# Moving a graph kernel's self loop from TensorE products to GpSimd edits of the resident adjacency

## What is computed

```
L0: dis*(adj @ (dis*h)) - h + sigmoid(alpha) * (softmax(beta*cosine*adj) @ h - h)
L1: (adj @ h + beta*h) / (deg + beta) @ kernel + bias
L2: relu((adj + I) normalised by its row sums @ (h @ W) + b)      <- the self loop I
L3: h_mul(concat(h, exp_map(adj @ log_map(h_mul(h, embed) + ...))), layer) + ...
```

## Time and profile before

| | |
|---|---|
| median of 3 runs | 905.12 us |
| the profiled execution | 904.95 us, of which 903.2 us is its span |
| TensorE busy | 849.7 us (94%) |
| VectorE, ScalarE, GpSimd busy | 626.5, 487.1, 289.5 us |
| mean granted TensorE clock | 0.991 of full speed |

### The profile page before, as it was taken

One profiled execution on the slowest core, in us unless ns is written; L12 is line 12 of the kernel. 1 busy time (PEld: TensorE's weight loads), 2 busy tenths in 40 slices (PEclk: granted clock), 3 DMA queues, 4 the chain that ended last, 5 costly groups with the idle time before them and its releaser, 6 DMA issues.

```text
span 903.2 us, 18349 instructions
## 1 busy us (share of the span) xinstructions
PE 849.7 (94%) x6464; PEld 510.3 (57%) x6464; DVE 626.5 (69%) x1775; ACT 487.1 (54%) x1027; POOL 289.5 (32%) x381
## 2 busy tenths in 40 slices
PE   0699999999999999999999999999999999999992
PEld 0366777777777777654444455555455555555451
DVE  6989999999999999953444313313147676637776
ACT  5878888888888886731222111111055566434543
POOL 6844444444654464531221100000022131213221
PEclk9999999999999999999999999999999999999997
DMA  8999999999999994000000000000000000000000
GB/s 262 223 224 271 234 269 232 282 232 254 258 271 249 240 249 111 2 1 1 1 1 0 1 1 1 1 1 1 1 1 1 1 1 1 1 1 25 24 24 25
DMA packets 96080, 89.79 MB, mean 99 GB/s; under 512 B 74368, under 2 KB 79616, under 8 KB 96000
## 3 DMA queue, kind: packets, MB, share of 16 engines
q1 hardware_dynamic: 92352, 88.11, 41.2%
q10 hardware_dynamic: 3648, 0.61, 0.4%
HBM read 69.81 MB, written 2.10 MB: 80 GB/s over the span
## 4 chain that ended last, share of the span: by engine, by line
PE 70%; DVE 15%; issue 6%; ACT 3%; DVEq 2%; POOL 2%; DMA 1%; ACTq 1%; SPq 0%; POOLq 0%
PE ps_acc L1353 28%; PE ps_acc L1264 16%; PE ps_s L1247 10%; PE ps_t L1353 6%; PE ps_t L1247 5%; DVE e_parts L803 2%; DVE ps_s L796 2%; POOL att_sb L385 1%; ACT e_parts L612 1%; DVE adj_t L735 1%; PE ps_s L1383 1%; PE ps_s L1415 1%; DMA x<-in_x 1%; PE ps_acc L1341 1%; ACT ez L571 1%
## 5 line engine op out<-in xcount | busy, mean ns | idle before, releaser
L334 POOL CAST e_parts<-ez 128x512 f16<-128x512 f32 x256 | 158.2, 645 | 177.5 <-ACT ez L483 116.1
L1264 PEld LDWEIGHTS ps_acc<-h_a,e_parts 128*128 128x128 f16 x3072 | 185.8, 97 | 34.4 <-DVE e_parts L803 4.2
L1264 PE MATMUL ps_acc<-h_a,e_parts 128*128 128x129 f16 x3072 | 197.4, 219 | 2.5 <-DVE e_parts L803 2.3
L1353 PE MATMUL ps_acc<-adj_t,stage 128*128 128x512 fp8e4 x896 | 198.6, 379 | 0.0
L803 DVE TENSOR_TENSOR e_parts<-ez,e_parts 128x512 f16<-128x512 f32 x256 | 180.0, 744 | 1.0 <-POOL e_parts L334 1.0
L1353 PE MATMUL ps_acc<-adj_t,h_a 128*128 128x512 fp8e4 x768 | 170.3, 379 | 0.0
L1353 PEld LDWEIGHTS ps_acc<-adj_t,stage 128*128 128x128 f16 x896 | 87.1, 98 | 99.1
L1247 PE MATMUL ps_s<-u_t 128*128 128x512 f16 x534 | 132.3, 385 | 9.0 <-ACT ez L483 7.3
L458 ACT ACTIVATE bytes<-stage 128x1024 uint8<-128x1024 f32 x128 | 133.8, 1046 | 0.9 <-DVE x L764 0.7
L483 ACT ACTIVATE ez<-ps_s,scal 128x1024 f32<-128x1024 f32 x89 | 107.1, 1203 | 44.4 <-DVE ps_s L796 43.3
L571 ACT ACTIVATE ez<-x,small 128x128 f32 (+1 forms) x96 | 39.6, 482 | 155.4 <-DVE small L980 155.4
(11 more groups left out here) (157 smaller groups left out, 814.4 us busy)
## 6 DMA issues: line engine op xcount, KB each, us to landing
stage<-in_adj SPq DMA_DIRECT2D x128, 512.0 KB, 5.0
x<-in_x SPq DMA_DIRECT2D x4, 512.0 KB, 8.5
adj_t<-bytes SPq DMA_TRANSPOSE x128, 5.1
out<-x SPq DMA_DIRECT2D x8, 256.0 KB, 2.2
kernel_sb<-in_L_gnn_kernel ACTq DMA_DIRECT2D x1, 64.0 KB, 7.1
w_sb<-in_L_gnn_W ACTq DMA_DIRECT2D x1, 64.0 KB, 8.1
embed_top<-in_L_gnn_embed ACTq DMA_DIRECT2D x1, 64.0 KB, 8.4
embed_top<-in_L_gnn_layer ACTq DMA_DIRECT2D x1, 64.0 KB, 7.3
```

The costliest lines, as they stand in the source:

```text
L334: g.tensor_copy(e_parts[:, HI, at, :], ez[:, at, :]).then_inc(ehi_done, 1)
L1264: last = t.matmul(att_acc[:, b, 0:D + 1], e_parts[:, re, g_s % RING, P * b:P * (b + 1)], h_a[:, s, rh, 0:D + 1], start=(s == 0 and n == 0 ...
L1353: last = t.matmul(acc, h[:, k, r, :], adj_f8[:, k // 2, CW * c:CW * (c + 1), k % 2], start=(k == 0 and r == LO), stop=(k == NB - 1 and r = ...
```

## The change

The products with `ident16x2` are taken out of `aggregate`. GpSimd adds the identity times 2.0 to the diagonal blocks of `adj_f8` after layer 1 has read them, so that an entry on the diagonal becomes 4.0, and subtracts it after layer 2 has read them. Each chunk is four GpSimd operations of 128 by 128 with an fp8 input and output and an fp16 identity. TensorE waits for the add at quarter (c, c) of layer 2, and for the subtraction at quarter (c, c) of layer 3. Two of GpSimd's loops on the chip become lists written out.

```diff
-            with pool.Fori(0, NCH) as m:
+            def self_loops(m, op, done):
+
+                for b in range(BC):
+                    k = BC * m + b
+                    own = adj_f8[:, k // 2, P * k:P * (k + 1), k % 2]
+                    last = g.tensor_tensor(own, own, ident16x2[:, :], op, saturate=False)
+                last.then_inc(done, 1)
+
+            for m in range(NCH):
                 rstd(NCH + m)
+                pool.wait_ge(agg_done, NCH + m + 1)
+                self_loops(m, ALU.add, loop_in)
...
-            with pool.Fori(0, NCH // 2 - 1) as i:
+            for i in range(NCH // 2 - 1):
                 roots_of_pair(i)
                 for par in (0, 1):
                     rstd(2 * NCH + 2 * i + 2 + par)
                     root_h(2 * i + 2 + par, par)
+                    pool.wait_ge(agg_done, 2 * NCH + 2 * i + par + 1)
+                    self_loops(2 * i + par, ALU.subtract, loop_out)
             roots_of_pair(NCH // 2 - 1)
+            pool.wait_ge(agg_done, 3 * NCH)
+            for m in (NCH - 2, NCH - 1):
+                self_loops(m, ALU.subtract, loop_out)
...
-                if L == 2 and q == NB // BC - 1:
-
-                    for b in range(BC):
-                        for r in (LO, HI):
-                            t.matmul(acc[:, P * b:P * (b + 1)], h[:, BC * c + b, r, :],
-                                     ident16x2[:, :], start=False, stop=False,
-                                     skip_group_check=True)
+                if L >= 2 and q == c:
+
+                    pe.wait_ge((loop_in, loop_out)[L - 2], c + 1)
```

More of the change, by code:

```diff
@@ L206, in program @@
                  "h_sq_in n_h_ok v_sq_in n_v_ok h2_sq_in n_h2_ok a_sq_in n_a_ok cat_sq_in "
-                 "n_cat_ok tanh_in tanh_out ln_in ln_out h2_ok v_ok v_out split_g diag_hi diag_ok "
+                 "n_cat_ok tanh_in tanh_out ln_in ln_out h2_ok v_ok v_out split_g loop_in loop_out diag_hi diag_ok "
                  "x_less x_att").split()
@@ L217, in program @@
          h_sq_in, n_h_ok, v_sq_in, n_v_ok, h2_sq_in, n_h2_ok, a_sq_in, n_a_ok, cat_sq_in,
-         n_cat_ok, tanh_in, tanh_out, ln_in, ln_out, h2_ok, v_ok, v_out, split_g, diag_hi,
+         n_cat_ok, tanh_in, tanh_out, ln_in, ln_out, h2_ok, v_ok, v_out, split_g, loop_in, loop_out,
+         diag_hi,
          diag_ok, x_less, x_att) = (
```

## The result

| | before | after |
|---|---|---|
| median of 9 runs each | 905.34 us | 903.24 us |
| ratio, 95% interval | | 0.9978 [0.9969, 0.9988] |
| the profiled execution / its span | 904.95 / 903.2 us | 903.19 / 901.2 us |

The change takes 0.22% off the time, with an interval of 0.12 to 0.31%. The forecast was 903.7; the median lies 0.46 under it, inside the range of 902.4 to 905.7, but outside the 903.4 to 904.4 that the prediction called the forecast itself. As a gain it is 2.0 us where 1.4 was forecast.

What follows compares the result with a forecast made beforehand. In layer 2 a circle through VectorE, ScalarE and GpSimd, with TensorE only in `prepare`, was taken to lead. The sum was 904.95 - 1.78 (removal) + 0.35 (collision) = 903.52 us, median 903.7, range 902.4 to 905.7.

Steps and rivals of the forecast that it cites:

- the forecast itself: Whole kernel: the median to expect lies between 903.4 and 904.4 us; chance 0.49.
- Only four of eight groups count: Layer 2, TensorE: removing identity products pays for chunks 0, 1, 2 and 7 only, 1.78 us; chunks 3 to 6 give nothing.
- VectorE's pass stays at 35.07: Layer 2: VectorE's pass over two chunks still takes 35.07 us after the change.
- The gap before `prepare(3)` grows to 1.2 us, and its start moves by 1.34: Layer 2, TensorE: it waits about 1.2 us there instead of 0.31, and the step at 711.34 moves by 1.34.
- The edit takes 0.35 us: GpSimd: one fp8 operation of 128 columns takes 0.35 us, between bounds of 0.28 and 0.56.
- The edits for an odd chunk cost nothing: Layer 2: VectorE's 2.37 us of idle time behind the root covers four operations of up to 0.56 us.
- The additions in layer 1 cost nothing: Layer 1: GpSimd's additions may delay VectorE, with 14 us of cover for at most 4 x 0.56 us.
- The collision at layer 3's start costs 0.35: Last eight GpSimd operations meet VectorE's small ones: VectorE loses 1.4 us, of which 1.05 is covered; loss 0.35 us.
- The room: Layer 3's start: VectorE's last split ends at 802.08, TensorE needs it at 803.13, 1.05 us later.
- no collision, or one inside the room: Rival, layer 3's start: GpSimd's last operations cost VectorE nothing that counts, so four groups pay in full: 903.3 us; chance 0.17.
- VectorE shut out until the last edit: Rival, layer 3's start: GpSimd's eight operations lock VectorE out throughout, costing 1.75 us: 905.1 us; chance 0.12.

Runs made afterwards that it cites:

- e2: Kernel before without the identity products of chunks 3, 4, 5 and 6, no edits on GpSimd; 905.69 us, ratio 1.0003 to before, distance on TensorE +0.02 us.
- e3: Kernel before without the identity products of chunks 0, 1, 2 and 7, no edits on GpSimd; 903.34 us, ratio 0.9982 to before, distance on TensorE -1.77 us.
- e10: Changed kernel with the last eight edits (chunks 6 and 7) held back until VectorE's last split of layer 2 is done; 903.6 us, ratio 0.9983 to before.
- e6: Changed kernel with two more GpSimd operations ahead of each chunk's four edits, written to a spare tile; 904.64 us, ratio 0.9997 to before.
- e11: e10 with ScalarE's loop of three passes in layer 2 written out; 900.72 us, ratio 0.9952 to before.
- e12: Kernel before with ScalarE's loop in layer 2 written out and nothing else; 903.84 us, ratio 0.9986 to before.
- e1: Kernel before without all eight groups of identity products in layer 2, no edits on GpSimd; 903.33 us, ratio 0.9983 to before.
- e4: Changed kernel with the identity products kept as well, so layer 2's self loop counts twice; 906.07 us, ratio 1.0008 to before.
- e5: The changed kernel again, nothing else altered; 903.4 us, ratio 0.9983 to before.
- e8: Changed kernel with prepare(3) and prepare(5) one quarter later in TensorE's list; 904.73 us, ratio 0.9994 to before.
- e7: Changed kernel with the last eight edits moved behind the first roots of layer 3, the roots' loop written out; 904.63 us, ratio 0.9995 to before.
- e9: Changed kernel with four more GpSimd operations ahead of each chunk's four edits, written to a spare tile; 908.97 us, ratio 1.0041 to before.

## Why the prediction was right, and where it was off

- **Only four of eight groups count.** Right, and shown by e2 and e3: +0.02 and -1.77 against 0 and -1.78.
- **VectorE's pass stays at 35.07.** It is 35.04, from these rows of VectorE after:

```profile
687.35 1.11 DVE L1119 SCALAR_TENSOR_TENSOR bytes<-ps_s,cols,bias_bc 128x128 f32<-128x128 f32 x4
...
722.39 1.12 DVE L1119 SCALAR_TENSOR_TENSOR bytes<-ps_s,cols,bias_bc 128x128 f32<-128x128 f32 x4
```

- **The gap before `prepare(3)` grows to 1.2 us, and its start moves by 1.34.** It is 1.17 late by the list (1.01 by the row's bracket) and moved by 1.51, of which 0.15 is the earlier start of the whole stretch.
- **The edit takes 0.35 us.** It takes 0.39: eight in a row last 3.12, four beside VectorE's small operations 1.58, and eight with VectorE idle 3.13 (e10). GpSimd's timeline of after:

```profile
697.74 2.07 POOL L403 TENSOR_TENSOR adj_t<-adj_t,ident16x 128x128 fp8e4<-128x128 fp8e4 x4
700.10 1.38 POOL L304 TENSOR_TENSOR small<-small,scal 128x4 f32<-128x4 f32 x1 [0.29 <-DVE small L984]
...
706.74 1.58 POOL L403 TENSOR_TENSOR adj_t<-adj_t,ident16x 128x128 fp8e4<-128x128 fp8e4 x4
...
793.85 3.12 POOL L403 TENSOR_TENSOR adj_t<-adj_t,ident16x 128x128 fp8e4<-128x128 fp8e4 x8
```

The block for an even chunk is the first row: it began beside VectorE's operation that ends at 698.37, and 1.44 us after that, at 699.81, it is through, close to the 1.40 that the prediction took. The root behind it was asked for 0.29 later and ended at 701.48, 0.53 before VectorE used it at 702.01. So the cost is nothing, with 0.29 + 0.53 = 0.82 us of cover for the root. e6 shows that this sum is not the whole margin: two more operations are 0.78 us, and its passes are 0.36 and 0.34 longer, 0.2 of it because VectorE's L994 itself stood behind an edit.

- **The edits for an odd chunk cost nothing.** Right: beside the block at 706.74 VectorE's L1039 took 0.39 and L1046 0.41 us instead of 0.17, but its idle time behind them, ended by ScalarE, shrank from the 2.37 of the earlier trace rows to 1.97 us.
- **The additions in layer 1 cost nothing.** Right. TensorE's timelines of before and of after, where layer 1 begins:

```profile
502.42 22.61 PE L1353 MATMUL ps_acc<-adj_t,h_a 128*128 128x512 fp8e4 x104
```

```profile
502.27 22.61 PE L1365 MATMUL ps_acc<-adj_t,h_a 128*128 128x512 fp8e4 x104
```

From there to 624.52 and to 624.37 it is 122.10 us in both.

- **The collision at layer 3's start costs 0.35.** This is the term that was mis-sized: VectorE's loss was put at 1.4 us and measured 1.04. The mechanism came as described, VectorE's timeline of after:

```profile
793.91 0.39 DVE L1039 TENSOR_SCALAR att_sb<-att_sb 128x8 f32<-128x8 f32 x1 [2.74 <-POOL att_sb L386]
...
794.76 0.20 DVE L1044 RECIPROCAL att_sb<-att_sb 128x8 f32<-128x8 f32 x1
795.05 0.40 DVE L1046 SCALAR_TENSOR_TENSOR att_sb<-att_sb 128x8 f32<-128x8 f32 x1
...
796.57 0.42 DVE L1056 SCALAR_TENSOR_TENSOR att_sb<-att_sb 128x8 f32<-128x8 f32 x1
...
797.31 0.69 DVE L1150 TENSOR_TENSOR ez<-ez,att_sb 128x512 f32<-128x512 f32 x1
...
800.44 0.69 DVE L1002 TENSOR_TENSOR h_a<-ez,h_a 128x512 f16<-128x512 f32 x1
```

Its stretch lasts 801.13 - 793.91 = 7.22 us, against 6.18 in e10 and before. It lost 1.04 us, not 1.4, because it was held up six times and not eight, by 0.17 on average: the reciprocals (L1044 above), for one, took 0.20 with and without the edits. The room was 1.05, so the loss just fits. TensorE's block of 24 took 5.39 instead of 5.34 (5.34 in e10, too), so 0.05 came through, not 0.35.

- **The number.** What came true at layer 3's start is the rival *no collision, or one inside the room*, put at 903.3 with a chance of 0.17; the median is 903.24. For the profiled execution the sum gave 903.52, and 903.19 was measured, 0.33 less. Of this 0.30 is the collision. Another 0.27 came off by the start of the stretch (0.15), the tail (0.07) and 0.05 in the stretch, all of the size of the scatter, and 0.24 came on outside the span, for which the prediction had no term. That these last nearly cancel is luck. The other 0.13 of the 0.46 is the distance from the profiled execution to its median: 0.17 was taken, it is 0.05 in after.

- **VectorE shut out until the last edit** (the rival with the lock in its harshest form) did not come: 3.12 us of edits back to back cost it 1.04. The Trainium skill (SBUF — State Buffer, Who interferes with whom) calls the port an exclusive lock whose loser blocks fully. The rows agree for a VectorE instruction that meets one edit (L1039, 0.39 instead of 0.17); by them VectorE gets its turn between two edits, and some of its instructions, such as L1044, are not held up at all.

## What to carry to other kernels

A busy share of 99.8% does not make an engine the bound: look for the one step at which it stands waiting, however short, because a circle through the other engines that is just as long as its list will swallow whatever you take out of the list. Sort the work that a change removes by whether it lies inside such a circle, and test it by taking out one half at a time (e2 and e3). Then look for what can leave the circle; here that was a table load, worth 0.80 us before the change and 2.6 after it.

## What the runs showed of the hardware

- The loop on the chip costs ScalarE a table load of 1.28 us ahead of its first plain copy in a pass; in the written-out passes it is absent (L594 with its load at 707.89 and without one at 777.75 above, L595 in e11). That it is the loop which makes the load necessary is shown by e11 and e12; why it stands just there was not tested.
- VectorE operations on eight columns with one tensor input are held up by a running GpSimd operation too: L1039 took 0.39 us beside the edits, and 0.17 in e10 (L1040 there), where there were none. Not all are: the reciprocal L1044 took 0.20 beside them, as in e10.
- GpSimd is held up as well: the block of four at 697.74 took 2.07 us. VectorE had begun an operation of 512 columns at 697.68 that lasts 0.69, to 698.37. The block at 706.74 met only operations on eight columns and took 1.58.
- The time outside the span is 0.2 us longer in after: 1.98 us as the mean of its nine executions, against 1.79 in before (35 executions beside e1 to e4) and in e12. It is 1.99 in e4, e5 and e8, 1.89 in e7 and 2.09 in e10 and e11. But it is 1.79 again in e6 and e9, which have all the edits and more operations on GpSimd. So it is not a price of each edit; what it comes from stays open.
